# GNN kernel: one-hot rings of the count stage eight units deep, and the former tile's list two units later

## The reference

```python
# layer 0
diff = edge_attr[:, None, :] - mu[None, :, :]
gauss = exp(sum(-0.5 * diff * diff / (EPS + sigma[None] ** 2), axis=-1))     # E x 3
msg = einsum('eko,ek->eo', (x[src] @ g).reshape(E, 3, 64), gauss)
aggr = segment_sum(msg, dst) / maximum(segment_sum(1, dst), 1)[:, None]
x = layernorm(x + silu(aggr + x @ root_w + bias + x))
# layers 1 and 2, over the same edges
nbr = segment_sum(h[src], dst) / maximum(deg, 1)[:, None]
h = h @ W_self + nbr @ W_neigh + b            # relu between the two
x = layernorm(x + h)
```

## Time and profile before

| | |
|---|---|
| median of 3 runs | 8203.81 us |
| the profiled execution's own time | 8277.25 us |
| its span, first to last instruction | 8275.3 us |
| mean granted TensorE clock, share of full | 0.761 |
| busy: DVE, PE, ACT, POOL | 61%, 58%, 45%, 40% |
| first stage's steps 3 to 97 | about 776 to 6770 us |

### The profile page before, as it was taken

One profiled execution on the slowest core, in us unless ns is written; L12 is line 12 of the kernel. 1 busy time (PEld: TensorE's weight loads), 2 busy tenths in 40 slices (PEclk: granted clock), 3 DMA queues, 4 the chain that ended last, 5 costly groups with the idle time before them and its releaser, 6 DMA issues.

```text
span 8275.3 us, 120249 instructions
## 1 busy us (share of the span) xinstructions
PE 4795.9 (58%) x21035; PEld 3512.1 (42%) x21036; DVE 5058.5 (61%) x14764; ACT 3721.3 (45%) x8949; POOL 3273.6 (40%) x3173
## 2 busy tenths in 40 slices
PE   1455555555545555445545555444444446999999
PEld 1123333333333433233333334333333335877777
DVE  4566566656555555556555656544454447888888
ACT  2212344444434343333433434344444434888887
POOL 3013455545554455445555545555555410000000
PEclk5557777777777777677767777777777767999999
DMA  2001111121111111112111111121211132777777
GB/s 66 26 15 30 46 44 43 42 49 42 42 42 41 46 44 42 29 40 50 42 46 45 42 49 42 41 50 42 50 42 41 41 62 80 254 251 244 247 249 224
DMA packets 498147, 612.98 MB, mean 74 GB/s; under 512 B 135126, under 2 KB 347652, under 8 KB 496916
## 3 DMA queue, kind: packets, MB, share of 16 engines
q1 hardware_dynamic: 392228, 495.60, 19.1%
q0 software_dynamic: 101568, 106.16, 7.3%
q10 hardware_dynamic: 4054, 8.11, 0.5%
HBM read 437.03 MB, written 172.56 MB: 74 GB/s over the span
## 4 chain that ended last, share of the span: by engine, by line
PE 23%; DVE 20%; issue 19%; another core or an unknown queue 13%; DVEq 12%; ACT 7%; DMA 4%; ACTq 1%; SPq 0%; POOLq 0%; POOL 0%
PE pw L904 8%; DVE rE L1412 4%; PE pw L1080 4%; PE pw L929 4%; DMA rA<-count 3%; ACT rE L611 3%; PE pw L1086 3%; DVEq L1622 3%; DVE rE L1472 2%; DVEq L1445 2%; ACT rB L650 2%; DVE rE L1410 2%; PE pw L876 2%; DVE rE L1540 1%
## 5 line engine op out<-in xcount | busy, mean ns | idle before, releaser
L548 POOL DMA_INDIRECT rE<-in_x,idx x3136 | 3238.4, 1033 | 3430.5 <-issue 3426.5
L650 ACT CAST rB<-pw 128x792 uint8<-128x792 f32 x1568 | 1258.7, 814 | 3797.6 <-remote 1104.1
L904 PE MATMUL pw<-rE 128*128 128x193 f32 x7824 | 1900.6, 411 | 1056.4 <-DVE rE L1472 911.6
L904 PEld LDWEIGHTS pw<-rE 128*128 128x128 f32 x7824 | 1749.4, 248 | 1281.8 <-DVE rE L1472 1046.8
L929 PE MATMUL pw<-rE 128*128 128x396 f16 x3840 | 869.0, 377 | 939.9 <-DVE rE L1412 374.2
L611 ACT ACTIVATE rE<-rE,cols 128x64 f32<-128x64 f32 x4704 | 1257.9, 344 | 31.8 <-issue 23.0
L1412 DVE TENSOR_SCALAR rE<-iperm,gr 128x392 f16<-128x392 f16 x3840 | 1075.8, 320 | 93.6 <-issue 90.8
L754 ACT ACTIVATE aring<-rA,scl 128x1024 fp32r<-128x1024 uint8 (+2 forms) x800 | 1026.2, 1327 | 217.7 <-DMA rA<-count 200.1
L1843 DVE TENSOR_SCALAR dring<-rA,scl 128x2048 fp32r<-128x2048 uint8 (+2 forms) x800 | 914.5, 1177 | 160.3 <-DMA rA<-count 142.2
L929 PEld LDWEIGHTS pw<-rE 128*128 128x128 f16 x3840 | 385.9, 107 | 1348.8 <-issue 676.9
L923 PE MATMUL pw<-rE 128*128 128x396 f16 x1600 | 394.1, 368 | 770.4 <-ACT rB L650 352.6
(11 more groups left out here) (271 smaller groups left out, 3088.9 us busy)
## 6 DMA issues: line engine op xcount, KB each, us to landing
rA<-count SPq DMA_DIRECT2D x672, 384.0 KB, 3.9
count<-rB SPq DMA_DIRECT2D x98, 1344.0 KB
rE<-in_x,idx POOLq DMA_INDIRECT x3136
rA<-count SPq DMA_DIRECT2D x96, 448.0 KB, 4.2
count<-rB SPq DMA_DIRECT2D x110, 224.0 KB, 2.2
cols<-cols_d SPq DMA_DIRECT2D x98, 64.0 KB
rA<-count SPq DMA_DIRECT2D x28, 192.0 KB, 2.5
cols_d<-rA SPq DMA_DIRECT2D x3, 1568.0 KB, 5.2
```

Of the source, the lines that this page charges most:

```text
L548: pool.indirect_dma_start(out=gath[:, s, u * CB + b, :], out_offset=None, in_=x, in_offset=bass.IndirectOffsetOnAxis(ap=idx[:, s, u * CB + ...
L650: act.copy(stage[:, s, :, j * 2 * W:(j + 1) * 2 * W].rearrange("p h (w n) -> p w h n", w=2), pu[j % 3][:, :, 0:CW].rearrange("p w (h n) -> ...
L904: ins = pe.matmul(sums[side][:, 0:AW], onehot[:, side, bb, :], wgath[:, side, bb, :], start=(bb == 0), stop=(bb == CB - 1))
```

## The change

`RU` goes from 4 to 8: both rings have 16 places, so eight units fit, or four units of two pairs. `comp` moves from `rE` to the upper half of `rB` (`RU * 4 * CW // 2` = 6336 words, exactly the two free quarters); the low one-hots stay in `rE` where `comp` began. Its constant columns are therefore set after the setup's last use of `rB`, and POOL's clearing of the third quarter waits for `s_bound`, the end of the steps. `LATE = 4` moves the list: behind unit 3 in merged and one-pair steps (so behind chunk 0), behind unit 1 in two-pair steps (just ahead of chunk 0). PE then waits for ACT's copy of unit 2, which shares the bank with `extra`, before the list, and for `x_add` before unit 5.

```diff
-RU = 4
+RU = 8
 U = 4
+LATE = 4
...
-        comp = rE[:, o:o + RU * 4 * CW // 2].bitcast(F16)...
-        o_lo = o + RU * 4 * CW // 2
+        comp = rB[:, HP * P // 2:HP * P // 2 + RU * 4 * CW // 2].bitcast(F16)...
+        o_lo = o
...
+            pool.wait_ge(s_bound, 1)
             pool.memset(rB[:, 2 * HP * P // 4:3 * HP * P // 4], 0.0).then_inc(f_clr, 1)
...
-                        if late and n == 2:
+                        at = LATE // max(1, pairs_w) - 1
+                        if late and n == (at + 3) // 3 * 3 - 1:
                             pe.wait_ge(x_add, pe.snap(xk, min_val=1, max_val=1 << 24))
                             pe.sem_inc(s_tick[0], 1)
                         unit(t, n, pairs_w)
-                        if late and n == 2 // max(1, pairs_w) - 1:
+                        if late and n == at:
+                            if at > 2:
+                                pe.wait_ge(a_evac, t * NU + 5)
+                                pe.sem_inc(s_tick[0], 1)
                             listed(other)
...
-                        free = n + 1 if behind < 2 else max(n + 1, min(n + 3, 4))
+                        free = n + 1 if behind < 2 else max(n + 1, min(RU // 2 + 1 + n // 2, RU))
                         dve.wait_ge(a_used, q * NU + free)
...
-                        if n == 1:
+                        if n == LATE - 1:
                             listed(q - 1, other)
...
-                        if late and n == 2 // pairs_w - 1:
+                        if late and n == LATE // pairs_w - 1:
                             listed(q - 1, other)
```

More of the change, by code:

```diff
@@ L125, in gnn_kernel @@
         o += 2 * CB * P
-        comp = rE[:, o:o + RU * 4 * CW // 2].bitcast(F16).rearrange("p (r b c) -> p r b c", r=2 * RU, b=2)
-        o_lo = o + RU * 4 * CW // 2
+        comp = rB[:, HP * P // 2:HP * P // 2 + RU * 4 * CW // 2].bitcast(F16).rearrange("p (r b c) -> p r b c", r=2 * RU, b=2)
+        o_lo = o
         lo1h = rE[:, o_lo:o_lo + RU * 4 * P // 2].bitcast(F16).rearrange("p (r c b) -> p r c b", r=2 * RU, b=2)
@@ L1348, in _ @@
             V.tensor_scalar(win_p[:], iota[:, 0:JW], float(GW * P), None, ALU.mult)
-            V.memset(comp[:].rearrange("p r b c -> p (r b) c")[:, :, GW:CW], 0.0)
             V.memset(scl[:, 0:2], 1.0)
@@ L1355, in _ @@
             link(V.memset(scl[:, 3:4], 65536.0))
-            V.memset(comp[:].rearrange("p r b c -> p (r b) c")[:, :, GW:GW + 1], 1.0 / 16)
-            V.memset(comp[:].rearrange("p r b c -> p (r b) c")[:, :, GW + 1:GW + 2], 1.0 / 2048)
             V.memset(gr[:], -1.0e6)
@@ L1365, in _ @@
             dve.wait_ge(s_evv, done_dve(FIELDS * QUADS - 1))
+            V.memset(comp[:].rearrange("p r b c -> p (r b) c")[:, :, GW:CW], 0.0)
             link(V.memset(rA[:], 0.0))
+            V.memset(comp[:].rearrange("p r b c -> p (r b) c")[:, :, GW:GW + 1], 1.0 / 16)
+            V.memset(comp[:].rearrange("p r b c -> p (r b) c")[:, :, GW + 1:GW + 2], 1.0 / 2048)
             dve.sem_inc(a_add, 1)
```

## The result

The changed kernel takes 8439.5 us (median of 4 runs, 8437.7 to 8478.6), the kernel before 8202.4 beside it (4 runs, 8198.5 to 8227.1): ratio 1.029, 95% interval 1.026 to 1.033. Forecast were 8120 and a range up to 8320; it is slower by 237 us and outside the range.

What follows compares the result with a forecast made beforehand. No engine was full; each step was taken as a chain of hand-overs between engines. Terms -150 + 70 + 13 - 20 + 2 = -85 us, off the median 8203.81, gave about 8120 us, range 7980 to 8320 (8 in 10).

Steps and rivals of the forecast that it cites:

- part 6: SP's column, index and store issue some 6 us later each step: no cost while POOL's slack covers it.
- Part 1, the rings: Rings of eight units remove DVE's waits on a full ring: -150 us, ends 0 and -381.
- less than 60 of 187: Sign in two-pair steps: DVE's idle time before L1410 that PE ends falls from 187 us to under 60.
- Parts 2 to 4, the list: Moving the list later: +70 us in merged steps, +13 in one-pair steps, -20 in two-pair steps.
- The walk: Step-by-step timing of PE, DVE and ACT around the moved list, giving the +70, +13 and -20 us.
- rival A: Slower: PE and DVE now meet behind chunk 0, whose length is unpredictable; +140, about 8345 us; chance 0.27.
- Part 4: Two-pair steps, list behind unit 1 instead of unit 0: a unit less between list and chunk 0; -20 us.
- Part 5, the new wait of PE: PE's wait for ACT's copy of unit 2 before the list: counted within the list's timing, no separate size.
- Part 7: Setup and end: memsets only move, POOL's clearing now runs behind the last steps; +2 us.
- B: No change: DVE's ring waits only move to before L1392 and the list; 8180 to 8230 us; chance 0.20.
- C: Larger gain: PE stands less mid-step, so its granted clock rises; -255, about 7950 us; chance 0.08.
- Rows 7 of the forecast: Trace of a chunk on PE, read as taking up to 11.6 us instead of 2.90, by ACT's and DVE's releases.

Runs made afterwards that it cites:

- e1: Changed kernel, with SP's index load moved ahead of its wait for the list's bound: ratio 0.957 to the kernel before.
- e4: Kernel before, with SP's index load moved ahead of its wait for the list's bound: ratio 0.969 to the kernel before.
- e3: Changed kernel with DVE's lead held to four units as before, so the list's new place alone: ratio 1.041 to the kernel before.
- e17: Kernel before with rings of eight, list at its old place, plus a POOL pause of 1.9 us after each eight gathers: 7280 us, ratio 0.886.
- e18: Kernel before, plus a POOL pause of 1.9 us after each eight gathers: ratio 0.894 to the kernel before.
- e6: Changed kernel with the list back at its old place and SP's index load ahead of its wait for the bound: ratio 0.952 to the kernel before.
- e7: Changed kernel, with POOL waiting for landing after each eight gathers instead of after all 32: ratio 0.895 to the kernel before.
- e10: Kernel before with rings of eight, list at its old place, and POOL waiting for landing after each eight gathers: ratio 0.893.

## Why the prediction was wrong

*The step that failed is part 6*: "SP issues columns, indices and the store some 6 us later in each step ... Nothing, as long as a step's slack of POOL covers 6 us". The delay is larger than that: the index load stands 13.8 us into a merged step instead of 4.9 and 27.3 us into a one-pair step instead of 11.7 (medians, from PE's first unit). Still the slack did cover it: ACT waits for no gather in the changed kernel. What I costed was the lateness of the data, and what it costs is the pattern of issue: POOL stands at the start (19.84 us above), catches up in longer unbroken series (78 of 24 or more against 27), and these slow the other engines' sequencers, 878 register instructions over 0.5 us against 596. By e1 against the change, late indices cost 1.029 - 0.957 = 7.2%; in the kernel before (e4) 3.1% were already being paid. The difference, 4.1%, some 340 us, is more than the whole loss of 237. The 1.029 is from another chip than e1 and e4, but on theirs the late list alone (e3) also costs 4.1%. The prediction read POOL's row for its busy share alone.

*Part 1, the rings.* DVE's waits went as forecast: what PE or "remote" ended at the ring fell from 381.5 us (in the three stretches) to 43.4 + 38.5 + 6.8 and two more of "remote" of 2 each. In two-pair steps I asked for less than 60 of 187; the first stretch has 78.8 left with "remote" counted, 38.5 without. The size was half: 0.99 is 84 us and e17 against e18 65, for 150 forecast and ends 0 and 381. The rest only moved to the waits behind.

*Parts 2 to 4, the list.* The walk gave +63 us, 0.8%. Without late indices the list's place has 0.5% (e1 against e6), with POOL's waits 0.2% (e7 against e10), both within the noise and each on two chips; e1 against e4, on one, leaves nothing for it. So the walk's 63 us are neither confirmed nor excluded. Its details held in merged steps, by PE's timelines: 2.0 us before chunk 0 (under 3 forecast, 5.5 before), 2.8 before unit 4 (some 3), 2.3 before chunk 1 (some 2), and 5.0 before the list's addition, up from 2.2. The last is under the 6 us set for rival A, and so is the mean over all steps, 4.1. Part 4 had the wait wrong: in two-pair steps PE's wait before unit 1 went from 5.6 us to nothing, but the one before chunk 0 rose from 0.6 to 9.4. Up to chunk 0, PE stands 19.9 us a step instead of 15.8, though the step as a whole became shorter.

*Part 5, the new wait of PE* is seen as L870's 72.7 us for ACT in 98 steps, inside the walk. *Part 7* never mattered.

*The rivals.* A had the sign, and at 8345 us came nearest, but its mechanism is refuted by e1 against e4; the range ended at 8320, below A's own price. B was right that part 1 mostly moves: 0.990 is not far from it. C had the chance 0.08 and needs less standing of PE; the granted clock stayed (0.761, 0.766). It rose in the faster forms, with early indices (0.809 in e1, 0.797 in e4) as with breaks each eight (0.805 to 0.824), but not with breaks each four or sixteen (0.780, 0.779). Rows 7 of the forecast, PE's matmuls released 7.7 us after their recorded end, were most likely a trace of the true cause, and I took them for long chunks. POOL's timeline has a series of 16 gathers there, from 5936.27 to 5957.65, and in the kernel before, 410 of the 492.8 us that "remote" ended before the chunk's addition ended with POOL past the eighth gather of a series or within 4 us behind it.

**What stays open.** Which part of the chip POOL's gathers share with the other sequencers, no run shows. Nor why e4 gains with more long series than before (late in them, at gathers 17 to 24, its share of slow instructions is 8.8%, where the changed kernel has 24.1%), or why the changed order costs 1.3% at series of sixteen: that it matters beside which work a series runs is argued, not shown. That PE's late releases and the slow register instructions have one cause rests on their going together (e7), not on a run that parts them. The slow register instructions alone are too few: at some 0.6 us each (697 less 85 ns) the 282 more of the changed kernel are about 170 us and the 510 fewer of e7 about 310, of 237 and 1076 us, and spread over two engines. And a break also spreads the gathers over the step (between two steps POOL stands 3.8 us in e7, 17.8 in the changed kernel); no run spreads them without breaks.

## What to carry to other kernels

A change that moves a small wait can change when another engine issues, and in what bursts; look at the moved queue's pattern of issue, not only at its slack and busy share. Where an untouched loop of tiny instructions shows more "issue" idle time, compare the duration of its register instructions with what POOL does in the same microseconds. Long series of indirect gathers want a short break, here about every eight; with fewer breaks the others are slowed, with more POOL becomes the bound.

## What was unexpected of the hardware

- In a series of back-to-back gathers (0.94 us each and 0.30 between them), ACT's register instructions took 697 ns in the median late in a series of 24, and 85 behind it. Of ACT's and DVE's together, under 0.5% are slow in the first four gathers of a series, 3 to 4% in the next four, and half from the 25th on (changed kernel). With a landing wait each four, 5 instructions of ACT and DVE are over 0.5 us; each eight, 275 to 368; each sixteen, 491 and 693; each 32, 596 and 878.
- A pause of POOL of 1.9 us that asks for no landing is enough: 0.910 in the changed kernel, which without a pause has 1.029. No pile of gathers on the way explains it: the last packet of a series starts 1.2 us after its last gather's record ends, in series of 8, 24 and 32 alike.
- POOL's writes in the pause are not free to DVE: it is busy 5319.4 us in e17 and 5042.8 in the changed kernel, 5289.8 in e18 and 5058.5 in the kernel before, with the same number of instructions.
